# One silu over two neighbouring PSUM banks in a macaron block (FFN, attention, FFN) on one core

## The reference

```python
# x: 2048 tokens of width 128; 64 experts of width F = 64, top 8
x = x + 0.5 * ffn(layernorm(x))
x = x + attention(layernorm(x))     # one head, 2048 x 2048 logits, softmax, scaled
x = x + 0.5 * ffn(layernorm(x))

# ffn, for all tokens and all 64 experts:
h = silu(einsum('td,edf->etf', x, W_up))
y = einsum('etf,efd->etd', h, W_down)
out = silu(x @ Ws_up) @ Ws_down + einsum('etd,te->td', y, cw)   # cw: sigmoid weights of the top 8, else 0
```

## Time and profile before

| what | value |
|---|---|
| time, median of 3 runs | 541.9 us (540.75 to 543.68) |
| profiled execution, its own time | 541.02 us |
| its span | 539.2 us |
| PE busy | 532.0 us, 99% |
| PE weight loads busy | 437.2 us, 81% |
| DVE busy | 408.5 us, 76% |
| ACT busy | 407.0 us, 75% |
| POOL busy | 273.7 us, 51% |
| granted TensorE clock | 1.00 |

### The profile page before, as it was taken

How to read it: one execution, slowest core, us unless ns; L and a number is a source line. 1 busy time by engine, 2 the same in 40 slices (tenths; PEclk the granted TensorE clock), 3 DMA queues, 4 the chain that set the end, 5 groups by cost and what they waited for, 6 DMA issues and landing times.

```text
span 539.2 us, 8716 instructions
## 1 busy us (share of the span) xinstructions
PE 532.0 (99%) x2710; PEld 437.2 (81%) x2710; DVE 408.5 (76%) x933; ACT 407.0 (75%) x815; POOL 273.7 (51%) x242
## 2 busy tenths in 40 slices
PE   8999999999999999999999999999999999999997
PEld 6677887887888888799999999878887888788886
DVE  5998689877966677867777889779678767965664
ACT  6898778877877775866666657778779777877773
POOL 3689757775776764000000000267676676766663
PEclk9999999999999999999999999999999999999999
DMA  8675555554555550000000000155565565556662
GB/s 264 194 220 200 189 182 167 179 197 150 172 187 193 190 160 1 2 1 0 1 2 1 2 1 0 50 193 171 166 195 169 168 202 169 182 157 204 202 193 84
DMA packets 44270, 72.25 MB, mean 134 GB/s; under 512 B 8864, under 2 KB 9632, under 8 KB 44224
## 3 DMA queue, kind: packets, MB, share of 16 engines
q1 hardware_dynamic: 43568, 71.17, 42.0%
q10 hardware_dynamic: 592, 0.39, 0.3%
q0 software_dynamic: 64, 0.13, 0.1%
HBM read 69.57 MB, written 2.10 MB: 133 GB/s over the span
## 4 chain that ended last, share of the span: by engine, by line
PE 93%; DVE 3%; ACT 2%; issue 1%; POOL 0%; DVEq 0%; POOLq 0%
PE lrow L1174 13%; PE lrow L1175 13%; PE lrow L1176 13%; PE bank L1216 11%; PE bank L1218 10%; PE bank L1217 10%; PE bank L1279 5%; PE bank L1501 3%; PE bank L1503 3%; PE bank L1502 3%; PE bank L1393 1%; PE bank L1286 1%; PE bank L1175 1%; PE bank L1176 1%; PE bank L1174 1%
## 5 line engine op out<-in xcount | busy, mean ns | idle before, releaser
L295 POOL TENSOR_TENSOR gpart_lo<-gated,gpart_hi 128x512 fp32r<-128x512 f32 x174 | 223.7, 1295 | 162.9 <-ACT gpart_hi L462 161.3
L451 ACT ACTIVATE lrow<-lrow 128x512 f32<-128x512 f32 (+1 forms) x245 | 143.9, 587 | 62.4 <-PE lrow L1176 61.9
L718 DVE TENSOR_TENSOR gated<-lrow,wide 128x512 f32<-128x512 f32 x170 | 116.1, 683 | 56.3 <-ACT lrow L451 53.6
L462 ACT CAST gpart_hi<-gated 128x512 fp32r<-128x512 f32 x174 | 106.7, 613 | 5.9 <-DVE gated L718 5.3
L1216 PE MATMUL bank<-gpart_lo,wdn_hi 128*128 128x512 f32 x246 | 97.7, 397 | 0.0
L1218 PE MATMUL bank<-gpart_hi,wdn_hi 128*128 128x512 f32 x246 | 97.7, 397 | 0.0
L1217 PE MATMUL bank<-gpart_hi,wdn_lo 128*128 128x512 f32 x246 | 97.0, 394 | 0.0
L718 DVE TENSOR_TENSOR lrow<-lrow,wide 128x512 f32<-128x512 f32 x74 | 51.4, 695 | 26.9 <-ACT lrow L451 26.9
L1092 DVE TENSOR_TENSOR pT_lo<-bank,pT_hi 128x512 fp32r<-128x512 f32 x64 | 43.6, 683 | 21.7 <-ACT pT_hi L650 21.7
L295 DVE TENSOR_TENSOR gpart_lo<-lrow,gpart_hi 128x512 fp32r<-128x512 f32 (+1 forms) x83 | 56.5, 681 | 1.6 <-ACT gpart_hi L462 1.3
L650 ACT CAST pT_hi<-bank 128x512 fp32r<-128x512 f32 x64 | 38.1, 595 | 24.1 <-PE bank L1279 23.9
(11 more groups left out here) (281 smaller groups left out, 978.2 us busy)
## 6 DMA issues: line engine op xcount, KB each, us to landing
wide<-gates_dram SPq DMA_DIRECT2D x488, 128.0 KB, 3.0
raw<-in_w_up SPq DMA_DIRECT2D x8, 256.0 KB, 5.5
raw<-in_w_down SPq DMA_DIRECT2D x8, 256.0 KB, 5.7
gates_dram<-gates SPq DMA_DIRECT2D x8, 128.0 KB, 2.3
x<-in_x SPq DMA_DIRECT2D x3, 256.0 KB, 3.9
out_dram<-x SPq DMA_DIRECT2D x3, 256.0 KB, 3.1
x<-in_x SPq DMA_DIRECT2D x1, 128.0 KB, 2.3
x<-in_x ACTq DMA_DIRECT2D x1, 128.0 KB, 2.5
```

What stands on the lines that cost most here:

```text
L295: return eng.tensor_tensor(gpart[1][0:m, U % NGP, :], gated_at(U)[0:m, :], gpart[0][0:m, U % NGP, :].bitcast(F32), ALU.subtract)
L451: nc.scalar.activation(dst[0:m, :], hid[U % NH][0:m, :], ACT.Silu).then_inc(s_silu, 1)
L462: nc.scalar.copy(gpart[0][0:m, U % NGP, :], gated_at(U)[0:m, :]).then_inc(s_ghi, 1)
L718: nc.vector.tensor_tensor(gated_at(U), a, b, ALU.mult).then_inc(s_gated, 1)
```

## The change

From unit 7 of each chunk on, ACT takes the silu of units u and u+1 (u odd) with one instruction on 128 x 1024, over two neighbouring banks of `lrow`, and adds 2 to the semaphore that counts silus. It waits for both up products, and stands behind hi(u-1) where the silu of unit u stood before it. So that units u and u+1 lie in neighbouring banks, the first FFN's banks are shifted by one: `hid_of(U)` takes the place of `U % NH`. With that, unit 29 of chunk 3 sits in bank 2 and unit 32 in bank 1, and the order in which the first token tile's logits banks are written and read becomes 2, 0, 1, 3.

```diff
--- before.py
+++ after.py
@@ -213,7 +213,7 @@
 
         def nth_logits(t, j):
 
-            return KB * t + ((1, 0, 2, 3), (1, 2, 3, 0))[t][j] if t < 2 else KB * t + j
+            return KB * t + ((1, 2, 0, 3), (1, 2, 3, 0))[t][j] if t < 2 else KB * t + j
 
         def values(c, h):
 
@@ -268,6 +268,10 @@
                 return u > EARLY and u % 2 == 1
             return u == 15 or u % 3 != 0 and (u < UNITS - 1 or n % NCH < NCH - 1)
 
+        def hid_of(U):
+
+            return (U + 1 - U // (NCH * PAIRS + 1)) % NH
+
         def lows(U, pool):
 
             return sum(on_pool(w) == pool for w in range(U + 1))
@@ -286,7 +290,7 @@
                 return wide[:, slot_of(EARLY, NCH), :]
             if on_pool(U):
                 return gated[:, (lows(U, True) - 1) % NG, :]
-            return hid[U % NH]
+            return hid[hid_of(U)]
 
         def low_part(eng, U):
 
@@ -441,14 +445,21 @@
                 U = place(u, n)
                 m = P if u else F
                 act.wait_ge(s_hid, U + 1)
-                dst = hid[U % NH] if u or n == 0 else gated_at(U)
+                dst = hid[hid_of(U)] if u or n == 0 else gated_at(U)
                 if early_unit(u, n):
                     if nth_gated(u, n) > NB:
                         act.wait_ge(s_gated, nth_gated(u, n) - NB)
                     dst = wide[:, slot_of(u, n), :]
                 if n == NCH and u == EARLY:
                     wait_low(act, place(0, n))
-                nc.scalar.activation(dst[0:m, :], hid[U % NH][0:m, :], ACT.Silu).then_inc(s_silu, 1)
+                nc.scalar.activation(dst[0:m, :], hid[hid_of(U)][0:m, :], ACT.Silu).then_inc(s_silu, 1)
+
+            def silu_pair(u, n):
+
+                U = place(u, n)
+                act.wait_ge(s_hid, U + 2)
+                two = lrow[:, hid_of(U) * CH:(hid_of(U) + 2) * CH]
+                nc.scalar.activation(two, two, ACT.Silu).then_inc(s_silu, 2)
 
             def hi_unit(u, n):
                 U = place(u, n)
@@ -587,10 +598,12 @@
                             pro_cwT(n)
                             silu_unit(3, n)
                     for u in range(7 if n == NCH else min(c, 1), UNITS):
-                        if c or u >= LEADS[f]:
+                        if u <= EARLY and (c or u >= LEADS[f]):
                             silu_unit(u, n)
                         if c or u > 1 - f:
                             hi_unit(*before(u, n))
+                        if u > EARLY and u % 2 == 1:
+                            silu_pair(u, n)
                         if n == 0 and u % 2 == 0 and PRE + u // 2 < 2 * WP:
                             piece_hi(PRE + u // 2)
                         if c + 1 < NCH:
@@ -714,7 +727,7 @@
                     a, b = g, gate_bank(u, n)
                 else:
                     dve.wait_ge(s_wide[slot_of(u, n)], 32 * landed(u, n))
-                    a, b = hid[U % NH], g
+                    a, b = hid[hid_of(U)], g
                 nc.vector.tensor_tensor(gated_at(U), a, b, ALU.mult).then_inc(s_gated, 1)
 
             def lo_unit(u, n):
@@ -1064,7 +1077,7 @@
                             last_yb(1, n)
                             last_x(1, n, z_x)
                         if f == 0:
-                            max_bank(0, 1)
+                            max_bank(0, 2)
                             last_yb(0, n)
                             last_x(0, n, h_x)
                             last_stats(0, h_x, 1, h_st)
@@ -1077,7 +1090,7 @@
                             last_normed(1)
                             max_bank(0, 0)
                             last_lo(1)
-                            max_bank(0, 2)
+                            max_bank(0, 1)
                             link(max_bank(0, KB - 1))
                             row_max(0)
                             epi_proj_lo(1)
@@ -1184,7 +1197,7 @@
                 elif U >= NH:
                     wait_hid_free(pe, U - NH)
                 w = [a[:, (u - 1) * P:u * P] for a in wup] if u else wsup
-                product(hid[U % NH][0:P if u else F, :], w, [a[:, n % 2, :] for a in xnT[n // NCH]]).then_inc(s_hid, 1)
+                product(hid[hid_of(U)][0:P if u else F, :], w, [a[:, n % 2, :] for a in xnT[n // NCH]]).then_inc(s_hid, 1)
 
             def spread_gate(u, n):
 
@@ -1451,7 +1464,7 @@
                             if f == 0 and (u, h) == (31, 0):
                                 pe.wait_ge(e_prlo, 1)
                                 wait_hid_free(pe, place(29, n))
-                                logits(0, 1)
+                                logits(0, 2)
                             if f == 0 and (u, h) == (30, 1):
                                 pe.wait_ge(j_lo, joint(n + 1))
                                 pe.wait_ge(e_lo, c)
@@ -1467,7 +1480,7 @@
                             turn_half(1, n)
                             epi_proj(1)
                             turn_tokens(0, h_xT)
-                            logits(0, 2)
+                            logits(0, 1)
                             keep_warm(2, bank[1])
                             turn_tokens(1, e_xT)
                             keep_warm(1, bank[1])
```

## The result

The changed kernel takes 597.9 us (median, 597.0 to 600.0, 6 runs), the kernel before 541.35 in the same runs (540.75 to 543.68): ratio 1.1051, interval 1.1036 to 1.1067. The forecast was 584.0 in a range of 563 to 602. The profiled execution took 599.97 us with a span of 598.2, 59.0 us longer than that of before; it is 2.1 us above the median, and its first up product already ends 2.1 us later than before: the first transfer lands 0.4 us later, and from 9.0 to 12.4 us the granted clock is at its lower level. In experiments 3 and 8 one execution each ran in a slow state of the chip (654 us at a mean clock of 0.75, 745 at 0.66) and is left out of the ratio.

The account below looks back on a forecast made before the run. PE, 99% busy, was taken as the bound, to be overtaken by an ACT-DVE chain: chunk losses 42.4, less 1.8, plus 2.4, give 43.0 us on 541.0, so 584.0. Range 563 to 602; its own mechanism 574 to 594.

Parts of the forecast that it names:

- the bare cycle: One pair of units without inserted work, through ACT and DVE in turn: 2.86 us, against PE's 2.79.
- The chain with DVE's work in it: DVE work between gate(u) and gate(u+1), such as low parts, prologue and epilogue, lengthens the cycle by its own time.
- the rival in which a pair costs two silus: Silu pair on ACT lasts 1.17 us, two banks one after the other: 15 us more, 599; chance 0.10.
- the loss by chunk: From unit 10 to 32, each chunk loses chain minus PE's window, 3.4 to 7.4 us; sum 42.4 us.
- granted clock still 1.00: Sign expected in the profile after: the granted clock stays at 1.00.
- more than the chain: Rival: PE, stopped and started in order, hands its own delay to the next silu; up to 610 us, chance 0.07.
- From unit 7 to 9 free: The first pairs, 7 to 9, cost nothing, as PE has transposes of its own from unit 8 to 10.
- The 0.3 us forgiven at each chunk's end: Where single silus begin again, units 1 to 6, ACT catches up 0.3 us: -1.8 for six chunks.
- The two tails: At the two ends of an FFN the tail waits for unit 31, some 1.2 us each: +2.4 us.
- Slack is used up: PSUM banks give 2.4 us to spare, but even DVE units' banks nothing, so PE falls in step with the chain.
- no change: Rival: the 2.4 us of slack swallow each chunk's lag; 541 us, chance 0.04.
- half of it: Rival: slack is used once in each chunk, as the lo of even DVE units doesn't bind; 567 us, chance 0.13.

Follow-up runs that it names:

- experiment 3: Changed kernel with the silu pair moved ahead of hi(u-1) in ACT's loop: 561.53 us, ratio 1.0372 to the kernel before.
- experiment 8: On top of experiment 4, DVE's prologue and epilogue work of odd units from 7 on moved behind gate(u+1): 558.81 us, ratio 1.0325.
- experiment 1: Changed kernel with single silus in their old places, keeping only the bank shift and the new logits order: 541.39 us, ratio 1.0006.
- experiment 4: Changed kernel with DVE's lo(u-1) moved ahead of gate(u) at odd u from 7 on: 570.81 us, ratio 1.0549.
- experiment 5: Changed kernel with the low part of unit 18, from chunk 1 on, on POOL instead of DVE: 586.10 us, ratio 1.0833.
- experiment 7: On top of experiment 3, from unit 7 on low parts of even units on POOL, of odd ones on DVE: 556.12 us, ratio 1.0277.
- experiment 9: Experiment 7 and experiment 8 together, except unit 9's work, left in its place: 558.35 us, ratio 1.0322.
- experiment 6: Changed kernel with extra PE matmuls between up products of units 21 and 22, chunks 4 to 6: twelve 598.18 us, seven 593.07 us.
- experiment 2: Changed kernel with two single silus, each with its own signal, in the pair's place: 563.46 us, ratio 1.0395.

## Why the prediction was right, and what it missed

- **The bound and the price of the bare change.** PE was the bound, the shift is free (experiment 1), the pair lasts 1.01 us (1.00 predicted, 1.17 the rival), the bare cycle is 2.85 (2.86).
- **The chain with DVE's work in it.** Shown in the trace and by experiments 4 and 8. Cycles of chunk 2, predicted by the terms and measured: unit 9 4.07 and 4.09, 11 3.26 and 3.32, 13 4.25 and 4.40, 15 3.72 and 3.69, 17 4.10 and 4.09, 25 and 27 3.46 and 3.49. Three cycles don't fit: 19, 21 and 23 took 4.14, 4.61 and 3.24 us against 3.46, 3.8 (with 0.4 for the block of unit 20) and 2.86 by the terms. In experiment 5, without lo(18) and with the clock up, 21 and 23 are 3.81 and 2.85.
- **The range**: 597.9 us lies in 563 to 602, but not in the 574 to 594 that the prediction gave its own mechanism. The upper end was there for the rival in which a pair costs two silus, and a pair doesn't. So it is partly luck that the range held.
- **The size**: 43.0 us forecast, 56.6 measured by the medians. The step that was too small is the loss by chunk, 42.4 forecast and 50.0 measured. From unit 10 to 32, forecast and measured:

| chunk | 0 | 1 | 2 | 3 | 4 | 5 | 6 | 7 |
|---|---|---|---|---|---|---|---|---|
| forecast | 7.4 | 5.7 | 6.4 | 4.2 | 4.7 | 5.3 | 5.3 | 3.4 |
| measured | 7.4 | 6.6 | 7.7 | 3.3 | 7.6 | 7.2 | 7.2 | 3.2 |
| with seven extra matmuls | 7.4 | 6.7 | 7.7 | 3.3 | 5.0 | 5.6 | 5.6 | 3.2 |

The five chunks that came out above the forecast are those in which the clock fell, and where it was kept up (last row, chunks 4 to 6) the forecast holds to 0.3 us. The prediction had "granted clock still 1.00". It had waits of PE as part of the chain, but not that a single wait of 3.5 us changes the price of what follows. Three chunks gave 4.8 us; by that five are worth about 8, an estimate. Chunk 3 came out 0.9 below: its cycles add up to the 35.2 us of the forecast, but its last up product is 0.7 us further ahead of its pair than the one of unit 10 was.
- **The rival "more than the chain"** (0.07), PE handing its delay back, is the mechanism of this: it said that lo to up to silu leaves 0.2 us. Experiment 3 measured that loop at 3.46 against a cycle of 3.50, so it left 0.04, and with PE at half clock it was the longer one.
- **"From unit 7 to 9 free"** was too good. From unit 1 to unit 10, chunks 1 to 7 lost 4.0 us together: in chunk 1 the transposes at unit 8 wait 0.9 us for DVE's part of the attention weights, which stands behind gate(7), and in chunk 4 up products wait 0.2 and 1.0 us for DVE's low parts. The 0.9 us of chunk 3 were not followed. The 0.3 us forgiven at each chunk's end (-1.8) was never seen. The two tails cost 1.9 and 1.4 us against 2.4 for both. Together with the 7.6 us of the chunks, and less 0.5 that chunk 0 gave back ahead of unit 10, these are the 13.6 us by which the forecast was short, to 0.2 us.
- **"Slack is used up"**: right against the rivals "no change" and "half of it", but for a reason that was only half seen. The prediction had the bank of an even DVE unit return 0.3 us too late (5.2 us against 4.9), but priced the cycle by ACT's chain alone. The two in fact run side by side. With the first gone, 20 us stay lost (experiment 3), of which experiment 7 takes 5 away; with lo moved out of both, 29.5 stay (experiment 4), as DVE's prologue work still stands in the first.
- **The signs.** PE waited 34.3 us for low parts, as forecast (some 40), but only 6 us of that in chunk 0, where most was expected. 17.7 us are five waits at unit 22, so that one sign of being wrong, waits gathered at a few units, came half true: that is where the clock fell. gate(u) waited about 100 times and gate(u+1) never, and chunks 7 and 0 took 33.9 and 40.7 us, as forecast.
- **Large tiles.** The advice of the Trainium skill to use them ("Advanced Engine Details and Errata", section "The Read-Write Bubble") brings no gain here. By start-to-start times one wide silu takes 0.93 of ACT against 1.0 for two, 0.07 us; ACT's busy sum rose by 1.2 us.

Left open: what keeps experiment 7 at 556 us. Its loss lies mostly in the chunks with a prologue, 1.1 to 2.9 us each, and the tails, and moving DVE's work as in experiment 9 doesn't lessen it. The same split with single silus wasn't tried.

## What to carry to other kernels

Joining two small instructions saves issue time on the engine that runs them and delays everyone who waits for the first half. Before doing it, write the order of each engine from one joined instruction to the next and follow who waits for whom: if the next one stands behind work that needs the result of this one, the engines take turns, and what stands between in any of their programs adds up one to one, unless something as long runs beside it. When a chain is found, look for a second one through the buffers that is just as long, since removing the first alone gives only a part back (here 36 of 57 us). And look at what a wait does to the engine that waits: here five waits of 3.5 us each lowered its clock.

## What the runs showed of the hardware

- A silu of 128x1024 f32 over two neighbouring PSUM banks lasts 1.004 to 1.023 us in the changed kernel, against 0.58 for 128x512. The 512 columns more cost 0.43 us, about twice the 0.20 that 256 more cost within a bank: crossing the bank border costs nothing that shows.
- After PE had stood still for 3.5 us at unit 22, the clock was at the lower of its two levels (1.2 instead of 2.4 GHz) or soon fell to it, in all nine such places (five in the changed kernel, two in each run of experiment 6): matmuls of 512 columns started 0.43 us apart instead of 0.23, for 6 to 12 of them, and then were fast again without any change in the program. The Trainium skill ("TensorE: Matmul & The Clock Gate", section "Part 1: The HAM clock gate") says that the low clock is the default and activity lifts it; the trace agrees, and seven otherwise useless matmuls in the wait kept the level up.
- Shorter waits can do it too: after the ten waits of 1.9 to 2.3 us at unit 22 in experiments 2 and 4 the clock fell five times; chunks 5 and 6 of experiment 2, where it did once, have the same program. After waits of up to 1.6 us in the chunks it never did. A fall was worth about 1.6 us, by chunks 5 and 6 of experiment 2 and by experiment 6 (4.8 us in three places).
- The extra matmuls are plain f32 of 256 columns and each shows as two of 0.21 us, start to start, so that twelve took 5.0 us; in the attention's start six of the same records had taken 1.3 us, from which I had priced them at half.
